# Linear attention in a fused decoder layer: one function table for exp and log, softplus in one VectorE operation, two biases on TensorE, the division on GpSimd

## The chip, the cores and the metric

One core of one Trainium2 chip runs the whole program. The metric is the device time of one execution in microseconds (us), median of several runs. A difference of about 0.2% can be told from no change. Engines: TensorE (PE, its weight loads PEld), VectorE (DVE), ScalarE (ACT), GpSimd (POOL), SyncE (SP), which issues most DMAs.

## The reference

A decoder layer over x (64 sequences of 128 rows of 128 features, float32): linear attention, cross attention to a context, and a mixture of experts, each followed by add and layer norm. The change touches the linear attention alone:

```
q = softplus(x @ Wq.T + bq);  k = softplus(x @ Wk.T + bk);  v = x @ Wv.T + bv      # 16 heads of 8
kv = cumsum(k[:, :, None] * v[:, None, :]);  k1 = cumsum(k)                        # over the 128 rows
out = (q . kv) / (q . k1)
x = layernorm(x + out @ Wo.T + bo)
```

softplus(z) is computed as max(z, 0) + log(1 + exp(-|z|)).

## The kernel before

The three layers are three blocks, one after the other. The linear attention (L153 to L483) works through 32 steps of two sequences (u = 0, 1), software-pipelined by hand: in step t an engine works for pair t, t-1, t-2, t-3 or t-4, by what it does. Each engine has its own instruction list (`step` in its block); the lists meet by semaphores, and within a list the order is that of the code. X keeps the whole activation in SBUF; x_rows is a second copy of x, loaded pair by pair (L245), for the matmuls.

In step t

- TensorE turns x_rows (L436), multiplies by Wq and Wk with the bias in front as two matmuls of a row of ones with the bias, split in a high and a low float32r part (L442, L443, then the float32 matmul L444, 256 columns; per u), turns the attention output of pair t-3 (L450), makes v of pair t (L459) and the output projection of pair t-3 (L464, both 128 columns per u, into one PSUM bank ps_vy), then the running sums of pair t-1 by a triangular matrix: of k (L472) and of kv (L479, four matmuls of 512 columns). The hardware runs each float32 matmul as two records in the profile.
- ScalarE copies the turned x out of PSUM (L307), writes the two normalised outputs of pair t-4 (L310), copies the turned attention output (L322), then |z| (L327), exp (L330), max(z, 0) (L332, into pos) and log (L335) of pair t, and the copy of v (L339). Exp and log need different function tables, so the program holds an ACT_TABLE_LOAD ahead of each.
- VectorE multiplies q by the sums (L356, once per u), adds pos and log to qk (L368), computes the shift of the layer norm (L374), the denominators' product (L380), the sums over the head dimension (L385), the residual (L390, projection plus X), the reciprocal of the denominators (L395), the layer norm's statistics (L399, L409, L413, L415) and the division, a product with the reciprocal (L403, into att).
- GpSimd computes the power of -0.5 (L267), adds the output bias to X (L272) and the value bias to v (L275), and makes the products k*v (L283, once per u).

At step 5 SyncE also issues the loads of all later weights (L134 to L149), ahead of the x_rows of pair 6 (L245).

Of the kernel before, what the change touches and what calls it, by code (L numbers as in the profile page):

```python
# [152 lines left out]
def linear_attention(nc, X, lat, ident, tri, x, weights, biases, later):  # L153
# [11 lines left out]
    with ExitStack() as stack:  # L165
# [5 lines left out]
        b_v = room.sbuf("b_v", [P, D])  # L171
        ones = room.sbuf("ones", [1, P], F32R)
        b_o = room.sbuf("b_o", [P, D])
        x_rows = room.sbuf("x_rows", [P, 2, 2, D])
        turned = room.sbuf("turned", [P, 4, S])
        pos = room.sbuf("pos", [P, 2, 2 * QK])
# [35 lines left out]
        pos_ready, v_ready, vb_ready = room.sem("pos_ready"), room.sem("v_ready"), room.sem("vb_ready")  # L212
# [5 lines left out]
        bias_added, sum_ready = room.sem("bias_added"), room.sem("sum_ready")  # L218
# [35 lines left out]
        def _(pool):  # L254
# [3 lines left out]
            pool.wait_ge(bvo_loaded, 32)  # L258
            for n in range(4):
                pool.wait_ge(res_loaded[n], 16)  # L260

            def step(t, par):
                s1, s4 = t - 1, t - 4
                if here(s4):
                    pool.wait_ge(square_ready, s4 * 2 + 2)
                    wait(pool, x1_ready, s4 * 2 - 2)
                    nc.gpsimd.tensor_tensor(scale[:, par, :], square[:, par, :], half[:], ALU.pow  # L267
                                            ).then_inc(scale_ready, 1)
                if here(s1):

                    pair = X[:, bass.ds(s1 * 2 * D, 2 * D)]
                    nc.gpsimd.tensor_tensor(pair.rearrange("p (b d) -> p b d", b=2), pair.rearrange("p (b d) -> p b d", b=2),  # L272
                                            b_o[:].unsqueeze(1).broadcast_to([P, 2, D]), ALU.add).then_inc(bias_added, 1)
                    pool.wait_ge(v_ready, s1 + 1)
                    nc.gpsimd.tensor_tensor(v[:, 1 - par], v[:, 1 - par], b_v[:].unsqueeze(1).broadcast_to([P, 2, D]),  # L275
                                            ALU.add).then_inc(vb_ready, 1)
                    pool.wait_ge(vb_ready, s1 + 1)
                    pool.wait_ge(qk_ready, s1 + 1)
                    for u in range(2):
                        wait(pool, cum_psum, s1 * 2 - 1 + u)  # L280
                        k_u = qk[:, 1 - par, u, D:QK].rearrange("p (h d) -> p h d", h=H)
                        v_u = v[:, 1 - par, u].rearrange("p (h e) -> p e h", h=H)
                        nc.gpsimd.tensor_tensor(kv[:, u], k_u.unsqueeze(1).broadcast_to([P, E, H, E]),  # L283
                                                v_u.unsqueeze(3).broadcast_to([P, E, H, E]), ALU.mult
                                                ).then_inc(kv_ready, 1)
# [4 lines left out]
        def _(act):  # L290
# [3 lines left out]
            for b, n in ((b_v, 2), (b_o, 3)):  # L294
                act.dma_start(b[:], biases[n].rearrange("(o d) -> o d", o=1).broadcast_to([P, D])
                              ).then_inc(bvo_loaded, 16)
            for n in range(4):
                act.dma_start(X[:, n * QUART * D:(n + 1) * QUART * D].rearrange("s (b d) -> s b d", d=D),
                              x[n * QUART:(n + 1) * QUART].rearrange("b s d -> s b d")).then_inc(res_loaded[n], 16)
            act.wait_ge(wT_psum, 1)  # L300
            nc.scalar.copy(w[:], ps_t[:]).then_inc(wT_ready, 1)

            def step(t, par):
# [19 lines left out]
                if here(t):  # L323
# [7 lines left out]
                    wait(act, qk_ready, t - 1)  # L331
                    nc.scalar.activation(pos[:, par], ps_qk[:], ACT.Relu).then_inc(pos_ready, 1)  # L332
# [11 lines left out]
        def _(dve):  # L344
# [4 lines left out]
                                    ).then_inc(b_lo_ready, 1)  # L349

# [9 lines left out]
            def step(t, par):  # L360
# [3 lines left out]
                if here(s1):  # L364

                    dve.wait_ge(log_ready, s1 + 1)
                    wait(dve, den_psum, s1 - 1)
                    nc.vector.tensor_tensor(qk[:, 1 - par].rearrange("p u f -> p (u f)"), pos[:, 1 - par], log[:], ALU.add  # L368
                                            ).then_inc(qk_ready, 1)
# [16 lines left out]
                if here(s3):  # L386
                    dve.wait_ge(vy_psum, t + 1)
                    dve.wait_ge(bias_added, s3 + 1)
# [11 lines left out]
                if here(s2):  # L400
                    dve.wait_ge(inv_ready, s2 + 1)
                    wait(dve, aT_psum, s2)
                    nc.vector.tensor_tensor(att[:].rearrange("p u h e -> p u e h"), numden[:, :, 0:E, :],  # L403
                                            inv[:].unsqueeze(2).broadcast_to([P, 2, E, H]), ALU.mult
                                            ).then_inc(att_ready, 1)
# [15 lines left out]
        def _(pe):  # L421
# [5 lines left out]
            pe.wait_ge(b_lo_ready, 1)  # L427
            pe.wait_ge(ones_ready, 1)

            def step(t, par):  # L430
                s1, s3 = t - 1, t - 3
                if here(t):
# [6 lines left out]
                    wait(pe, pos_ready, t)  # L439
# [17 lines left out]
                if here(t):  # L457
                    for u in range(2):
                        last = nc.tensor.matmul(ps_vy[:, u * D:(u + 1) * D], turned[:, u, :], w[:, QK:3 * D],  # L459
                                                start=True, stop=True)  # L460
                if here(s3):
                    pe.wait_ge(aT_ready, s3 + 1)
                    for u in range(2):
                        last = nc.tensor.matmul(ps_vy[:, (2 + u) * D:(3 + u) * D], turned[:, 2 + u, :], w[:, 3 * D:4 * D],  # L464
                                                start=True, stop=True)
# [953 lines left out]
```

## Time and profile before

| | us |
|---|---|
| median of 3 runs (lowest, highest) | 2271.53 (2271.13, 2274.04) |
| the profiled execution | 2267.62 |
| its span on the core | 2265.6 |
| granted TensorE clock, mean over the span | 0.985 |

| engine | busy us (share of the span) |
|---|---|
| PE | 2163.8 (96%) |
| PEld | 1841.5 (81%) |
| DVE | 1575.9 (70%) |
| ACT | 1479.8 (65%) |
| POOL | 1386.0 (61%) |

The linear attention takes the first 322 us or so of the span; the cross attention starts its first matmul at 324.3 us. The shares above are means over three layers with different limits, so what the change is worth has to be read from the first 322 us alone. A clock of 1.0 is the 2.4 GHz level of TensorE, 0.5 the 1.2 GHz level.

### The profile page before, as it was taken

What the parts mean: (1) busy time and instruction counts of PE and PEld (TensorE: products, weight loads), DVE (VectorE), ACT (ScalarE), POOL (GpSimd) and SP (SyncE); (2) the same over time, 40 slices, a digit from 0 to 9 for tenths busy, and PEclk for the clock granted to TensorE, in tenths of its full rate; (3) what the DMA queues carried; (4) which work ended last, traced back from release to release, by engine and by line L of the source; (5) the groups of instructions that cost most, each with busy time, mean ns of one, the idle gap of its engine ahead of it and who ended that gap; (6) DMA issues with size and microseconds to landing.
All of it is one profiled execution on the core that took longest, in us unless ns stands there. A gap on an engine that the chain in (4) does not pass through costs nothing. (4 is left out here: it accounts for less than half of the span.)

```text
span 2265.6 us, 44642 instructions
## 1 busy us (share of the span) xinstructions
PE 2163.8 (96%) x16233; PEld 1841.5 (81%) x16233; DVE 1575.9 (70%) x3455; ACT 1479.8 (65%) x3820; POOL 1386.0 (61%) x1481
## 2 busy tenths in 40 slices
PE   6899967999999999999999999999989999999998
PEld 3455547999999999999999999999977777777776
DVE  3899965666666666666666666666657777777775
ACT  4788845667676666666676766666655665665664
POOL 4788856566565565565665655655654666666666
PEclk9999979999999999999999999999999999999999
DMA  3311110000000000000000000000000000000000
GB/s 93 113 33 33 30 30 5 6 10 6 10 7 6 10 6 6 11 6 6 11 6 10 7 6 10 6 6 10 6 1 1 10 5 10 10 5 10 10 5 14
DMA packets 52794, 33.46 MB, mean 15 GB/s; under 512 B 2968, under 2 KB 50274, under 8 KB 52450
## 3 DMA queue, kind: packets, MB, share of 16 engines
q1 hardware_dynamic: 50174, 26.30, 4.0%
q10 hardware_dynamic: 2404, 4.33, 0.7%
q8 instruction: 131, 2.15, 0.4%
q14 instruction: 85, 0.70, 0.1%
HBM read 22.22 MB, written 8.39 MB: 14 GB/s over the span
## 5 line engine op out<-in xcount | busy, mean ns | idle before, releaser
L653 POOL TENSOR_TENSOR x_prob<-x_prob,x_inv 128x496 f32<-128x496 f32 x514 | 521.7, 1015 | 546.9 <-DVE x_inv L792 546.9
L728 ACT ACTIVATE x_prob<-x_ps_S,x_nmax 128x248 f32<-128x248 f32 x1028 | 473.2, 468 | 130.4 <-DVE x_nmax L786 130.3
L786 DVE TENSOR_REDUCE x_nmax<-x_ps_S 128x2 f32<-128x496 f32 x515 | 345.5, 671 | 181.3 <-PE x_ps_S L491 181.1
L736 ACT COPY x_probT<-x_ps_T 124x512 f32<-124x512 f32 x512 | 300.7, 587 | 225.0 <-PE x_ps_T L955 225.0
L1117 POOL TENSOR_TENSOR e_hidden_lo<-e_hidden,e_hidden_hi 128x512 fp32r<-128x512 f32 x224 | 291.8, 1306 | 196.6 <-ACT e_hidden_hi L1161 195.7
L489 PE MATMUL x_ps_S<-x_kT_lo,x_G_hi 128*128 128x248 f32 x1030 | 329.6, 320 | 0.0
L955 PE MATMUL x_ps_T<-ident,x_prob 128*124 128x128 f32 x2048 | 315.1, 276 | 11.3 <-POOL x_prob L653 11.3
L955 PEld LDWEIGHTS x_ps_T<-ident,x_prob 128*124 128x124 f32 x2048 | 237.8, 139 | 71.7 <-POOL x_prob L653 29.2
L490 PE MATMUL x_ps_S<-x_kT_hi,x_G_lo 128*128 128x248 f32 x1030 | 287.3, 279 | 0.0
L491 PE MATMUL x_ps_S<-x_kT_hi,x_G_hi 128*128 128x248 f32 x1030 | 286.7, 278 | 0.0
L772 DVE TENSOR_TENSOR x_G_lo<-x_ps_G,x_G_hi 128x512 fp32r<-128x512 f32 x259 | 178.8, 690 | 129.2 <-ACT x_G_hi L722 129.1
L930 PE MATMUL x_ps_O<-x_probT,x_V 124*64 124x128 f32 x4096 | 251.8, 276 | 0.2 <-ACT x_probT L736 0.2
L930 PEld LDWEIGHTS x_ps_O<-x_probT,x_V 124*64 124x64 f32 x4096 | 220.9, 137 | 18.9 <-issue 5.1
L1172 ACT ACTIVATE e_silu<-e_ps_gate 128x512 f32<-128x512 f32 x224 | 134.5, 601 | 154.5 <-PE e_ps_gate L491 149.0
L722 ACT CAST x_G_hi<-x_ps_G 128x512 fp32r<-128x512 f32 x259 | 152.0, 587 | 91.6 <-PE x_ps_G L491 91.4
L728 ACT ACTIVATION_READ_ACCUMULATOR x_prob<-x_ps_S,x_nmax 128x1 f32 x1028 | 206.8, 201 | 0.0
L490 PEld LDWEIGHTS x_ps_S<-x_kT_hi,x_G_lo 128*128 128x128 f32 x1030 | 196.3, 191 | 0.0
L489 PEld LDWEIGHTS x_ps_S<-x_kT_lo,x_G_hi 128*128 128x128 f32 x1030 | 195.4, 190 | 0.0
L491 PEld LDWEIGHTS x_ps_S<-x_kT_hi,x_G_hi 128*128 128x128 f32 x1030 | 194.8, 189 | 0.0
L1257 DVE TENSOR_TENSOR e_act_up<-e_silu,e_ps_up 128x512 f32<-128x512 f32 x176 | 120.3, 684 | 90.2 <-PE e_ps_up L491 52.8
L778 DVE COPY x_V<-x_ps_V 124x512 f32<-124x512 f32 x259 | 176.6, 682 | 1.8 <-PE x_ps_V L491 1.8
L1161 ACT CAST e_hidden_hi<-e_hidden 128x512 fp32r<-128x512 f32 x224 | 137.4, 613 | 26.7 <-DVE e_hidden L1263 25.9
(199 smaller groups left out, 5135.3 us busy)
## 6 DMA issues: line engine op xcount, KB each, us to landing
x_nk<-latents SPq DMA_DIRECT2D x34, 124.0 KB
lin_x_rows<-in_x SPq DMA_DIRECT2D x32, 128.0 KB, 2.4
latents<-lin_nlat SPq DMA_DIRECT2D x32, 128.0 KB, 1.8
out_dram<-e_result SPq DMA_DIRECT2D x16, 256.0 KB, 2.2
x_nk<-in_ctx SPq DMA_DIRECT2D x34, 120.0 KB, 2.1
w_wkv<-in_L_xattn_Wkv SPq DMA_DIRECT2D x1, 1024.0 KB, 6.1
w_rows<-in_L_ffn_w_gate SPq DMA_DIRECT2D x1, 704.0 KB, 5.8
w_rows<-in_L_ffn_w_up SPq DMA_DIRECT2D x1, 704.0 KB, 6.2
```

What stands on the lines that cost most here:

```text
L489: nc.tensor.matmul(out, stationary[0], moving[1], start=first, stop=False)
L490: nc.tensor.matmul(out, stationary[1], moving[0], start=False, stop=False)
L491: return nc.tensor.matmul(out, stationary[0], moving[0], start=False, stop=last)
L653: nc.gpsimd.tensor_tensor(prob[:, k], prob[:, k], inv[:, k].unsqueeze(2).broadcast_to([P, 2, K]), ALU.mult).then_inc(prob_ready, 1)
L728: nc.scalar.activation(prob[:, k, h, :], ps_S[:, n % BANKS, h * K:(h + 1) * K], ACT.Exp, bias=nmax[:, k, h:h + 1], accum_out=total[:, k, h ...
L736: nc.scalar.copy(probT[0:KT, s % (2 * GANG)], ps_T[0:KT, s % 2, :]).then_inc(probT_ready, 1)
L772: nc.vector.tensor_tensor(G_part[1][:, pair].rearrange("p h u q -> p (h u q)"), ps_G[:], G_part[0][:, pair].bitcast(F32).rearrange("p h u ...
L778: nc.vector.tensor_copy(V[:, hf, u, tile, :], ps_V[0:KT, :]).then_inc(V_ready, 1)
L786: nc.vector.tensor_reduce(nmax[:, k, :], ps_S[:, n % BANKS, 0:2 * K].rearrange("p (h k) -> p h k", h=2), AX, ALU.max, negate=True).then_in ...
L930: last = nc.tensor.matmul(ps_O[h * DH:(h + 1) * DH, k * S:(k + 1) * S], V[:, j // 4, u, tile, (j % 4 * 2 + h) * DH:(j % 4 * 2 + h + 1) * D ...
L955: last = nc.tensor.transpose(ps_T[0:KT, s % 2, at:at + S], prob[:, s % RINGS, h, tile * KT:(tile + 1) * KT], ident[:])
L1117: nc.gpsimd.tensor_tensor(hidden_part[1][0:rows, n % RING, :], hidden[0:rows, n % 2, :], hidden_part[0][0:rows, n % RING, :].bitcast(F32), ...
```

## The change

1. ScalarE: one table that holds both exp and log is loaded ahead of the steps; the max(z, 0) pass (pos) is dropped.
2. VectorE: qk is one scalar_tensor_tensor, max(ps_qk, 0) + log, read straight from PSUM. TensorE's next product into ps_qk therefore waits for qk and not for pos.
3. The value and output biases leave GpSimd. They become two small matmuls per sequence (a row of ones by a 128-column part of the bias, high and low) ahead of each product, in the new `projected`. The two extra biases are split in the prologue on VectorE, which also waits for X there.
4. The division moves from VectorE in step t (pair t-2) to GpSimd in step t+1 (the same pair, now t-3), ahead of the power.

```diff
@@ -168,12 +168,11 @@
-        b_v = room.sbuf("b_v", [P, D])
+        b_vo = room.sbuf("b_vo", [1, 2, D])
+        b_vo_part = [room.sbuf(f"b_vo_{n}", [1, 2, D], F32R) for n in ("hi", "lo")]
-        b_o = room.sbuf("b_o", [P, D])
-        pos = room.sbuf("pos", [P, 2, 2 * QK])
...
@@ -255,26 +254,22 @@
             nc.gpsimd.memset(half[:], -0.5).then_inc(half_ready, 1)
             nc.gpsimd.memset(ones[:].bitcast(F32), 1.0).then_inc(ones_ready, 1)
             pool.wait_ge(half_ready, 1)
-            pool.wait_ge(bvo_loaded, 32)
-            for n in range(4):
-                pool.wait_ge(res_loaded[n], 16)
 
             def step(t, par):
-                s1, s4 = t - 1, t - 4
+                s1, s3, s4 = t - 1, t - 3, t - 4
+                if here(s3):
+                    pool.wait_ge(inv_ready, s3 + 1)
+                    wait(pool, aT_psum, s3)
+                    nc.gpsimd.tensor_tensor(att[:].rearrange("p u h e -> p u e h"), numden[:, :, 0:E, :],
+                                            inv[:].unsqueeze(2).broadcast_to([P, 2, E, H]), ALU.mult
+                                            ).then_inc(att_ready, 1)
                 if here(s4):
                     pool.wait_ge(square_ready, s4 * 2 + 2)
                     wait(pool, x1_ready, s4 * 2 - 2)
                     nc.gpsimd.tensor_tensor(scale[:, par, :], square[:, par, :], half[:], ALU.pow
                                             ).then_inc(scale_ready, 1)
                 if here(s1):
-
-                    pair = X[:, bass.ds(s1 * 2 * D, 2 * D)]
-                    nc.gpsimd.tensor_tensor(pair.rearrange("p (b d) -> p b d", b=2), pair.rearrange("p (b d) -> p b d", b=2),
-                                            b_o[:].unsqueeze(1).broadcast_to([P, 2, D]), ALU.add).then_inc(bias_added, 1)
                     pool.wait_ge(v_ready, s1 + 1)
-                    nc.gpsimd.tensor_tensor(v[:, 1 - par], v[:, 1 - par], b_v[:].unsqueeze(1).broadcast_to([P, 2, D]),
-                                            ALU.add).then_inc(vb_ready, 1)
-                    pool.wait_ge(vb_ready, s1 + 1)
                     pool.wait_ge(qk_ready, s1 + 1)
                     for u in range(2):
                         wait(pool, cum_psum, s1 * 2 - 1 + u)
@@ -291,12 +286,12 @@
             for n in range(2):
                 act.dma_start(b_qk[:, n * D:(n + 1) * D], biases[n].rearrange("(o d) -> o d", o=1)
                               ).then_inc(bqk_loaded, 16)
-            for b, n in ((b_v, 2), (b_o, 3)):
-                act.dma_start(b[:], biases[n].rearrange("(o d) -> o d", o=1).broadcast_to([P, D])
-                              ).then_inc(bvo_loaded, 16)
+            for n in range(2):
+                act.dma_start(b_vo[:, n, :], biases[2 + n].rearrange("(o d) -> o d", o=1)).then_inc(bvo_loaded, 16)
             for n in range(4):
                 act.dma_start(X[:, n * QUART * D:(n + 1) * QUART * D].rearrange("s (b d) -> s b d", d=D),
                               x[n * QUART:(n + 1) * QUART].rearrange("b s d -> s b d")).then_inc(res_loaded[n], 16)
+            nc.scalar.preload_act_table_set("natural_log_exp_and_others")
             act.wait_ge(wT_psum, 1)
             nc.scalar.copy(w[:], ps_t[:]).then_inc(wT_ready, 1)
 
@@ -328,8 +323,6 @@
                     act.wait_ge(mag_ready, t + 1)
                     wait(act, log_ready, t)
                     nc.scalar.activation(dec[:], mag[:], ACT.Exp, scale=-1.0).then_inc(dec_ready, 1)
-                    wait(act, qk_ready, t - 1)
-                    nc.scalar.activation(pos[:, par], ps_qk[:], ACT.Relu).then_inc(pos_ready, 1)
                     act.wait_ge(dec_ready, t + 1)
                     wait(act, qk_ready, t)
                     nc.scalar.activation(log[:], dec[:], ACT.Ln, bias=1.0).then_inc(log_ready, 1)
@@ -347,6 +340,13 @@
             dve.wait_ge(b_hi_ready, 1)
             nc.vector.tensor_tensor(b_qk_part[1][:], b_qk[:], b_qk_part[0][:].bitcast(F32), ALU.subtract
                                     ).then_inc(b_lo_ready, 1)
+            dve.wait_ge(bvo_loaded, 32)
+            nc.vector.tensor_copy(b_vo_part[0][:], b_vo[:]).then_inc(b_hi_ready, 1)
+            dve.wait_ge(b_hi_ready, 2)
+            nc.vector.tensor_tensor(b_vo_part[1][:], b_vo[:], b_vo_part[0][:].bitcast(F32), ALU.subtract
+                                    ).then_inc(b_lo_ready, 1)
+            for n in range(4):
+                dve.wait_ge(res_loaded[n], 16)
 
             def numerators(s, par, u):
 
@@ -365,8 +365,8 @@
 
                     dve.wait_ge(log_ready, s1 + 1)
                     wait(dve, den_psum, s1 - 1)
-                    nc.vector.tensor_tensor(qk[:, 1 - par].rearrange("p u f -> p (u f)"), pos[:, 1 - par], log[:], ALU.add
-                                            ).then_inc(qk_ready, 1)
+                    nc.vector.scalar_tensor_tensor(qk[:, 1 - par].rearrange("p u f -> p (u f)"), ps_qk[:], 0.0, log[:],
+                                                   ALU.max, ALU.add).then_inc(qk_ready, 1)
                 if here(s4):
 
                     dve.wait_ge(scale_ready, s4 + 1)
@@ -385,7 +385,6 @@
                     nc.vector.tensor_reduce(numden[:], prod[:], AX, ALU.add).then_inc(numden_ready, 1)
                 if here(s3):
                     dve.wait_ge(vy_psum, t + 1)
-                    dve.wait_ge(bias_added, s3 + 1)
                     wait(dve, x1_ready, (s3 - 1) * 2)
                     nc.vector.tensor_tensor(res[:, 1 - par], ps_vy[:, 2 * D:4 * D].rearrange("p (u f) -> p u f", u=2),
                                             X[:, bass.ds(s3 * 2 * D, 2 * D)].rearrange("p (u f) -> p u f", u=2), ALU.add
@@ -397,12 +396,6 @@
                     wait_apart(dve, b_lo_ready, (sum_ready, s3 + 1), (mom_ready, s3 * 2))
                     for u in range(2):
                         nc.vector.bn_stats(stat[:, u, :], res[:, 1 - par, u, :]).then_inc(stat_ready, 1)
-                if here(s2):
-                    dve.wait_ge(inv_ready, s2 + 1)
-                    wait(dve, aT_psum, s2)
-                    nc.vector.tensor_tensor(att[:].rearrange("p u h e -> p u e h"), numden[:, :, 0:E, :],
-                                            inv[:].unsqueeze(2).broadcast_to([P, 2, E, H]), ALU.mult
-                                            ).then_inc(att_ready, 1)
                 if here(s3):
                     for u in range(2):
                         wait_apart(dve, b_lo_ready, (stat_ready, s3 * 2 + u + 1))
@@ -424,8 +417,14 @@
                 last = nc.tensor.transpose(ps_t[:, n * D:(n + 1) * D], w_rows[:, n, :], ident[:])
             last.then_inc(wT_psum, 1)
             pe.wait_ge(wT_ready, 1)
-            pe.wait_ge(b_lo_ready, 1)
+            pe.wait_ge(b_lo_ready, 2)
             pe.wait_ge(ones_ready, 1)
+
+            def projected(out, n, rows, weight):
+
+                nc.tensor.matmul(out, ones[:], b_vo_part[1][:, n, :], start=True, stop=False)
+                nc.tensor.matmul(out, ones[:], b_vo_part[0][:, n, :], start=False, stop=False)
+                return nc.tensor.matmul(out, rows, weight, start=False, stop=True)
 
             def step(t, par):
                 s1, s3 = t - 1, t - 3
@@ -436,7 +435,7 @@
                         last = nc.tensor.transpose(ps_t[:, u * S:(u + 1) * S], x_rows[:, par, u, :], ident[:])
                     last.then_inc(xT_psum, 1)
                     pe.wait_ge(xT_ready, t + 1)
-                    wait(pe, pos_ready, t)
+                    wait(pe, qk_ready, t)
                     for u in range(2):
                         out = ps_qk[:, u * QK:(u + 1) * QK]
                         nc.tensor.matmul(out, ones[:], b_qk_part[1][:], start=True, stop=False)
@@ -456,13 +455,11 @@
                     pe.wait_ge(sum_ready, s3)
                 if here(t):
                     for u in range(2):
-                        last = nc.tensor.matmul(ps_vy[:, u * D:(u + 1) * D], turned[:, u, :], w[:, QK:3 * D],
-                                                start=True, stop=True)
+                        last = projected(ps_vy[:, u * D:(u + 1) * D], 0, turned[:, u, :], w[:, QK:3 * D])
                 if here(s3):
                     pe.wait_ge(aT_ready, s3 + 1)
                     for u in range(2):
-                        last = nc.tensor.matmul(ps_vy[:, (2 + u) * D:(3 + u) * D], turned[:, 2 + u, :], w[:, 3 * D:4 * D],
-                                                start=True, stop=True)
+                        last = projected(ps_vy[:, (2 + u) * D:(3 + u) * D], 1, turned[:, 2 + u, :], w[:, 3 * D:4 * D])
                 if here(t) or here(s3):
                     last.then_inc(vy_psum, 1)
                 if here(s1):
```

How the instructions move. On TensorE, in one steady step, from the end of the q and k products to the sums of k (L459 and L464 before are the products for v and for the output, L425 to L427 now the two bias matmuls and the product). Before:

```order
L450 MATMUL lin_ps_t<-ident,lin_att 128x128
L459 MATMUL lin_ps_vy<-lin_w,lin_turned 128x128 [waits lin_sum_ready,lin_v_ready]
L459 MATMUL lin_ps_vy<-lin_w,lin_turned 128x128
L464 MATMUL lin_ps_vy<-lin_w,lin_turned 128x128 [waits lin_aT_ready]
L464 MATMUL lin_ps_vy<-lin_w,lin_turned 128x128
L472 MATMUL lin_ps_den<-lin_qk,tri 128x256 [waits lin_den_taken,lin_qk_ready]
```

Now, on TensorE in the same place (line numbers of the changed kernel):

```order
L425 MATMUL lin_ps_vy<-lin_b_vo_lo,lin_ones 128x128 [waits lin_sum_ready,lin_v_ready]
L426 MATMUL lin_ps_vy<-lin_b_vo_hi,lin_ones 128x128
L427 MATMUL lin_ps_vy<-lin_w,lin_turned 128x128
L425 MATMUL lin_ps_vy<-lin_b_vo_lo,lin_ones 128x128
L426 MATMUL lin_ps_vy<-lin_b_vo_hi,lin_ones 128x128
L427 MATMUL lin_ps_vy<-lin_w,lin_turned 128x128
L425 MATMUL lin_ps_vy<-lin_b_vo_lo,lin_ones 128x128 [waits lin_aT_ready]
L426 MATMUL lin_ps_vy<-lin_b_vo_hi,lin_ones 128x128
L427 MATMUL lin_ps_vy<-lin_w,lin_turned 128x128
L425 MATMUL lin_ps_vy<-lin_b_vo_lo,lin_ones 128x128
L426 MATMUL lin_ps_vy<-lin_b_vo_hi,lin_ones 128x128
L427 MATMUL lin_ps_vy<-lin_w,lin_turned 128x128
```

Eight matmuls are added per step; the waits stay where they were.

On GpSimd, one steady step before (v of pair t-1, then its products k*v, then the power of the next step):

```order
L267 TENSOR_TENSOR lin_scale<-lin_square,lin_half 128x4 [waits lin_x1_ready,lin_square_ready]
L272 TENSOR_TENSOR X<-X,lin_b_o 128x256
L275 TENSOR_TENSOR lin_v<-lin_v,lin_b_v 128x256 [waits lin_v_ready]
L283 TENSOR_TENSOR lin_kv<-lin_qk,lin_v 128x1024 [waits lin_cum_psum,lin_qk_ready,lin_vb_ready]
L283 TENSOR_TENSOR lin_kv<-lin_qk,lin_v 128x1024 [waits lin_cum_psum]
```

The same step on GpSimd now:

```order
L263 TENSOR_TENSOR lin_att<-lin_numden,lin_inv 128x2x8x16 [waits lin_aT_psum,lin_inv_ready]
L269 TENSOR_TENSOR lin_scale<-lin_square,lin_half 128x4 [waits lin_x1_ready,lin_square_ready]
L278 TENSOR_TENSOR lin_kv<-lin_qk,lin_v 128x1024 [waits lin_cum_psum,lin_qk_ready,lin_v_ready]
L278 TENSOR_TENSOR lin_kv<-lin_qk,lin_v 128x1024 [waits lin_cum_psum]
```

The two bias additions are gone and the division stands first; the power stands between the division and the products as it stood ahead of the additions.

## Rows read from the trace of the kernel before

**Rows 1.** Busy time of each engine in one steady stretch of 60 us.

```profile
core 0: us, PE busy (x) PEld busy (x) DVE busy (x) ACT busy (x) POOL busy (x), PEclk, DMA share, GB/s
180.00:240.00 60.00, 55.16 (x213) 31.38 (x214) 59.48 (x107) 51.66 (x92) 50.77 (x37) 1.00 0.11 31
```

**Rows 2.** Timeline of one steady step, VectorE and GpSimd (start us, us, what).

```profile
212.38 1.22 DVE L356 TENSOR_TENSOR lin_prod<-lin_ps_cum,lin_qk 128x1024 f32<-128x1024 f32 x1
...
213.52 0.68 DVE L368 TENSOR_TENSOR lin_qk<-lin_pos,lin_log 128x512 f32<-128x512 f32 x1
213.55 1.24 POOL L272 TENSOR_TENSOR X<-X,lin_b_o 128x256 f32<-128x256 f32 x1
...
214.12 0.69 DVE L374 SCALAR_TENSOR_TENSOR lin_shift<-lin_mom,lin_scale 128x4 f32<-128x4 f32 x1
...
214.75 0.72 POOL L275 TENSOR_TENSOR lin_v<-lin_v,lin_b_v 128x256 f32<-128x256 f32 x1
...
215.55 4.23 POOL L283 TENSOR_TENSOR lin_kv<-lin_qk,lin_v 128x1024 f32<-128x1024 f32 x2
...
216.31 2.56 DVE L385 TENSOR_REDUCE lin_numden<-lin_prod 128x288 f32<-128x2304 f32 x1
...
219.71 0.61 DVE L403 TENSOR_TENSOR lin_att<-lin_numden,lin_inv 128x256 f32<-128x256 f32 x1
...
220.56 1.22 DVE L356 TENSOR_TENSOR lin_prod<-lin_ps_cum,lin_qk 128x1024 f32<-128x1024 f32 x1
...
221.75 1.25 DVE L368 TENSOR_TENSOR lin_qk<-lin_pos,lin_log 128x512 f32<-128x512 f32 x1
```

**Rows 3.** Timeline of TensorE, step 7 (from 86.29 to 94.42 us).

```profile
86.29 0.38 PE L436 MATMUL lin_ps_t<-ident,lin_x_rows 128*128 128x128 f32 x2
87.14 0.38 PE L442 MATMUL lin_ps_qk<-lin_b_qk_lo,lin_ones 1*128 1x256 f32 x1 [0.46 <-ACT lin_turned L307]
...
88.19 0.38 PE L442 MATMUL lin_ps_qk<-lin_b_qk_lo,lin_ones 1*128 1x256 f32 x1
88.42 0.28 PE L443 MATMUL lin_ps_qk<-lin_b_qk_hi,lin_ones 1*128 1x256 f32 x1
88.62 0.70 PE L444 MATMUL lin_ps_qk<-lin_w,lin_turned 128*128 128x256 f32 x2
89.16 0.38 PE L450 MATMUL lin_ps_t<-ident,lin_att 128*128 128x128 f32 x2
89.38 0.61 PE L459 MATMUL lin_ps_vy<-lin_w,lin_turned 128*128 128x128 f32 x4
90.00 0.71 PE L464 MATMUL lin_ps_vy<-lin_w,lin_turned 128*128 128x128 f32 x4
90.55 0.60 PE L472 MATMUL lin_ps_den<-lin_qk,tri 128*128 128x256 f32 x2
90.98 3.60 PE L479 MATMUL lin_ps_cum<-lin_kv,tri 128*128 128x512 f32 x8
94.42 0.38 PE L436 MATMUL lin_ps_t<-ident,lin_x_rows 128*128 128x128 f32 x2
```

**Rows 4.** Timeline of TensorE at the start of the last step, 31.

```profile
289.36 0.38 PE L436 MATMUL lin_ps_t<-ident,lin_x_rows 128*128 128x128 f32 x2
```

**Rows 5.** Groups of instructions, ScalarE, up to 322 us (busy us, mean ns).

```profile
L335 ACT ACT_TABLE_LOAD x32 | 41.1, 1283 | 0.6
L330 ACT ACT_TABLE_LOAD x31 | 39.8, 1283 | 0.6
```

**Rows 6.** Timeline of TensorE in the cross attention: float32r matmuls of 248 columns.

```profile
700.74 0.28 PE L490 MATMUL x_ps_S<-x_kT_hi,x_G_lo 128*128 128x248 f32 x1
700.86 0.28 PE L491 MATMUL x_ps_S<-x_kT_hi,x_G_hi 128*128 128x248 f32 x1
```

**Rows 7.** Timeline of SyncE's DMA issues around step 5 (start us, us, what).

```profile
56.09 0.50 SPq L245 DMA_DIRECT2D lin_x_rows<-in_x  x1
...
70.88 0.47 SPq L245 DMA_DIRECT2D lin_x_rows<-in_x  x1
```

**Rows 8.** Timeline of TensorE at the start of step 6.

```profile
75.06 0.66 PE L436 MATMUL lin_ps_t<-ident,lin_x_rows 128*128 128x128 f32 x2 [4.98 <-DMA lin_x_rows<-in_x]
76.18 0.58 PE L442 MATMUL lin_ps_qk<-lin_b_qk_lo,lin_ones 1*128 1x256 f32 x1 [0.46 <-ACT lin_turned L307]
```

More of the change, by code:

```diff
@@ L211, in linear_attention @@
         qk_psum, vy_psum = room.sem("qk_psum"), room.sem("vy_psum")
-        pos_ready, v_ready, vb_ready = room.sem("pos_ready"), room.sem("v_ready"), room.sem("vb_ready")
+        v_ready = room.sem("v_ready")
         mag_ready, dec_ready, log_ready = room.sem("mag_ready"), room.sem("dec_ready"), room.sem("log_ready")
@@ L217, in linear_attention @@
         numden_ready, inv_ready, att_ready = room.sem("numden_ready"), room.sem("inv_ready"), room.sem("att_ready")
-        bias_added, sum_ready = room.sem("bias_added"), room.sem("sum_ready")
+        sum_ready = room.sem("sum_ready")
         stat_ready, mom_ready = room.sem("stat_ready"), room.sem("mom_ready")
```

## Prediction

> **What bounds the kernel now.** The page first: its shares are means over three layers, so I cut out the linear attention with the windows view. In a steady 60 us VectorE is busy 59.48 us, TensorE 55.16, ScalarE 51.66, GpSimd 50.77, at clock 1.00 [rows 1]. VectorE looks like the only limit. The timeline says why it is so full: from one L356 to the next is 220.56 - 212.38 = 8.18 us, and part of that is waiting for GpSimd. L368 takes 0.68 us when it starts ahead of L272 and L272 then takes 1.24; at 221.75 it takes 1.25. L374, four elements wide, takes 0.69 and ends at 214.81, just after L272 does (213.55 + 1.24 = 214.79) [rows 2]. So two engines that both read SBUF with two inputs take turns.
>
> TensorE decides this case, though, and a busy share doesn't show how near it is to its own limit, since its records overlap. Starts do. In step 7, after a stall, every engine had caught up with its work and TensorE waits for nothing but the round trip through ScalarE's copy of x (0.46 us): that step takes 94.42 - 86.29 = 8.13 us [rows 3]. Piece by piece: turn and copy 0.85, q and k 2.02, turn 0.22, v 0.62, output 0.55, k sums 0.43, kv sums 3.44. From step 7 to step 31 there are 24 steps, (289.36 - 86.29)/24 = 8.46 us each [rows 3, 4]. The average step is thus VectorE's, and TensorE has 8.46 - 8.13 = 0.33 us of room in it. That 0.33 is all that may be added to TensorE for nothing, and all that making the others faster can win per step.
>
> **The change part by part.**
>
> *ScalarE.* 31 + 32 table loads of 1.283 us, 81 us in all, go, and the max pass with them [rows 5]: some 3.1 us of about 7.3 per step (51.66/60 x 8.46). ScalarE was not the limit; what it gives is that its copy of x is never late. The new table load in the prologue stands where one stood before. The copy's 0.85 stays in TensorE's chain, since the copy can't start before the turned x is there.
>
> *VectorE.* The division's 0.61 goes, the turns with GpSimd go at L368 (0.57 in every other step) and up to 0.55 at L374; the new qk reads PSUM, and I take the 0.68 of the old one for it. 8.46 - 0.5 - 0.3 - 0.5 is about 7.2 us per step. Splitting two more biases in the prologue lies beside the loading of X.
>
> *GpSimd.* L272 and L275 go (0.7 to 1.2 each, [rows 2]), the division comes, 256 elements like L275, so about 0.7: some 6 us per step. The division waits for the reciprocal of the step before and stands after k*v, which ends well before; queued behind it are the power and k*v. TensorE reads its result only after q and k of the same step, some 3 us in. Both have room.
>
> *TensorE.* Eight matmuls of one row by 128 columns per step. Their price is in no row as such, so I bound it. Nearest row: the same form with 256 columns. L442 to L443 is 0.23, L443 to L444 0.20; a whole sequence (two bias matmuls and L444) takes 88.19 - 87.14 = 1.05 and 89.16 - 88.19 = 0.97 [rows 3]. A float32 product of 256 columns alone takes 0.43 (L472 to L479), so a pair costs 0.62 and 0.54. That is the upper end with nothing taken off for half the columns: 4 x 0.58 = 2.3 us per step. A float32r matmul of 248 columns with the weights loaded beside another takes 0.12 [rows 6], half of that is 0.06: the lower end is 8 x 0.06 = 0.48. That the small matmuls cost nearly twice 0.12 here shows that the weight load of the row of ones isn't hidden, and that doesn't shrink with the columns. I take the pair at 0.58 less the streaming of 256 fewer columns in all, between 0.12 (one pass, rows 6) and 0.21 (two passes, as L472's 0.43 for two records of 256): 0.46 to 0.37, say 0.425, and 4 x 0.425 = 1.7 us per step. No engine hides it: these stand in TensorE's own list, and nothing below 0.48 is possible by any row here, which is already more than the 0.33 of room.
>
> The Trainium skill ("TensorE: Matmul & The Clock Gate", section "Back-to-back issue gap") gives about 81 ns for each matmul of 128 columns in a stream with its weight load. By that the eight would cost 0.65 us, and the step would be 8.78. The rows of the same form (0.20 to 0.23 for 256 columns) speak against it, as weights of one row don't seem to be pulled ahead here.
>
> *The step* becomes TensorE's: 8.13 + 1.7 = 9.83 us against 8.46, +1.37. The waits that bound steps before (for the copies, for k*v) are gone, for VectorE at 7.2 delivers early. The new wait of q and k for the old qk (instead of pos) falls due well before: qk comes 1.8 us after the first half of the kv sums, TensorE asks for it after the second half (1.7) and the turned x (0.85). SyncE is moved past nothing.
>
> **The sum.** Steps 7 to 30: 24 x 1.37 = +32.9. Step 31: +1.4. Steps 2 to 5 would bring about 5 more, but in step 6 TensorE waits 4.98 us for x_rows, which lands 75.06 - 56.09 = 18.97 us after the issue ahead of the weight loads, at step 4 [rows 7, 8]. That issue moves with step 4 by some 2 us only, so step 6 starts some 2 us late and most of the wait is used up. Step 6 itself took 86.29 - 75.06 = 11.23 us [rows 3, 8]; its matmuls are long (0.66 against 0.38) because the clock fell to 0.5 (1.2 GHz) after those idle 5 us. With about 1.5 us idle I expect it to stay at 2.4 GHz and step 6 to take 9.8: -1.4. Up to step 7 that makes +0.5. Filling and draining: the early and late steps lose table loads and gain bias matmuls; I take 0, +-3. Sum: 0.5 + 32.9 + 1.4 = +34.8. The profiled execution took 2267.6 (span 2265.6), so 2302.4; it was 3.9 below the median of the runs, so I put 2306.
>
> **The rivals.**
>
> *A, cheap bias matmuls (12%).* The weight load of the ones hides behind the product before. For it: in the cross attention such loads do hide [rows 6]. Against: [rows 3]. Step 8.61 to 8.78: 24 x 0.15 to 0.32 is +3.6 to +7.7, the start gives or takes 1: 2275 to 2280.
>
> *B, VectorE blocked by k*v (7%).* The new step has VectorE's shift right behind qk, and k*v starts on qk as well. If k*v gets in first, the shift (two SBUF inputs) waits out one product, 2.1 us (4.23/2), or both, and L356 behind it. By 2.1 VectorE needs 9.3, which hides; by 4.2, 11.4 us, +2.9 over 8.46: 24 x 2.9 is +70, 2341. Against: the shift is next on its own engine and k*v needs a semaphore; and GpSimd's list has the power ahead of k*v, so the scale is there. The Trainium skill ("SBUF — State Buffer", section "Who interferes with whom") has this rule, that issue order decides who blocks, for the whole instruction; rows 2 agree on who waits (L374 ends with L272).
>
> *C, faster (5%).* TensorE's 8.13 holds slack I don't see, as the eight matmuls fill gaps where it waits for weights or copies: the output part waits for the copy of att, the q part 0.46 us for that of x. This decides if the eight add less than 0.33 to the 8.13. At 0 the step is 8.13: -0.33 x 24 = -8, and with the start -1 to -3: 2261. For it: 0.46 us idle per step. Against: they stand behind q and k, not in that gap.
>
> *D, the table isn't shared or the loads stay (1%).* The built program holds one ahead of the steps. TensorE's sum would be the same.
>
> The forecast has the other 75%. Its own spread is the price of the eight: 1.3 to 2.3 per step gives 2296 to 2321. The range 2285 to 2321 leaves out A below, B and C. Faster or slower counts from 0.2% (4.5 us), about what a measurement of this kernel can tell: faster 0.05, same 0.04 (the low end of A), slower 0.91.
>
> **What would show it.** In the changed profile: steady starts of the x turning 9.8 us apart; L425 to L426 0.15 to 0.2 us, v and output together 2.9 instead of 1.17; VectorE's busy share in 180 to 240 down to about 45 us with idle time ended by PE, ScalarE's to about 30; no table load in the steps; no L374 over 0.2 us; the wait for x_rows in step 6 under 3 us and clock 1.0 there. The forecast is wrong if steps stay under 8.8 us (A) or if VectorE stays at 59 of 60 us (B).

## The result, and the profile after

| | before | changed |
|---|---|---|
| median us (lowest, highest), 4 runs each | 2272.78 (2271.13, 2274.05) | 2332.51 (2329.74, 2338.10) |
| profiled execution, its span | 2267.62, 2265.6 | 2331.12, 2329.4 |
| mean granted clock of the span | 0.985 | 0.976 |

The change makes the kernel slower: ratio 1.0266, 95% interval 1.0245 to 1.0288. The forecast had the sign and the engine, but put 2306 with a range up to 2321: +35 us where +60 came. One execution of e1 below, the profiled one, took 2730.38 us at a mean granted clock of 0.744; it is left out of e1's median and ratio, and no steps are read from it.

TensorE in one steady step of the changed kernel (start us, us, what), which answers to [rows 3]:

```profile
199.16 0.38 PE L435 MATMUL lin_ps_t<-ident,lin_x_rows 128*128 128x128 f32 x2
200.01 0.38 PE L441 MATMUL lin_ps_qk<-lin_b_qk_lo,lin_ones 1*128 1x256 f32 x1 [0.46 <-ACT lin_turned L302]
...
202.03 0.38 PE L449 MATMUL lin_ps_t<-ident,lin_att 128*128 128x128 f32 x2
202.34 0.32 PE L425 MATMUL lin_ps_vy<-lin_b_vo_lo,lin_ones 1*128 1x128 f32 x1
202.50 0.27 PE L426 MATMUL lin_ps_vy<-lin_b_vo_hi,lin_ones 1*128 1x128 f32 x1
202.70 0.49 PE L427 MATMUL lin_ps_vy<-lin_w,lin_turned 128*128 128x128 f32 x2
203.12 0.32 PE L425 MATMUL lin_ps_vy<-lin_b_vo_lo,lin_ones 1*128 1x128 f32 x1
...
205.38 0.60 PE L469 MATMUL lin_ps_den<-lin_qk,tri 128*128 128x256 f32 x2
205.81 3.60 PE L476 MATMUL lin_ps_cum<-lin_kv,tri 128*128 128x512 f32 x8
...
209.24 0.38 PE L435 MATMUL lin_ps_t<-ident,lin_x_rows 128*128 128x128 f32 x2
```

The step is 10.08 us. Its pieces are those of before but for two: from the first L425 to L469 now takes 3.04 us where v and output took 1.17, and the turn ahead of them 0.31 instead of 0.22. Sum: +1.96 us for eight small matmuls, 0.245 each. A second cost is seen only over several steps. Windows of TensorE's steps 17, 18 and 19, and of steps 7 to 30 together:

```profile
core 0: us, PE busy (x) PEld busy (x) DVE busy (x) ACT busy (x) POOL busy (x), PEclk, DMA share, GB/s
199.16:209.24 10.08, 9.62 (x39) 5.85 (x38) 7.46 (x15) 4.42 (x10) 5.97 (x4) 1.00 0.09 26
209.24:221.01 11.77, 11.31 (x40) 6.80 (x39) 7.46 (x15) 4.42 (x10) 5.96 (x4) 0.86 0.08 22
221.01:231.08 10.07, 9.61 (x39) 5.84 (x38) 7.45 (x15) 4.42 (x10) 5.97 (x4) 1.00 0.10 28
93.41:350.18 256.77, 245.69 (x914) 147.97 (x913) 178.92 (x335) 106.14 (x240) 143.07 (x96) 0.94 0.09 25
```

Same instructions, same order, but step 18 is 1.69 us longer because the clock was at 0.5 (1.2 GHz) for a part of it. Three windows of 1 us within it:

```profile
214.00:215.00 1.00, 1.00 (x7) 0.81 (x6) 0.00 (x0) 0.69 (x2) 0.00 (x0) 1.00 0.00 0
216.00:217.00 1.00, 1.00 (x3) 0.69 (x3) 1.00 (x5) 0.37 (x1) 0.32 (x1) 0.50 0.00 0
219.00:220.00 1.00, 1.00 (x4) 0.43 (x3) 0.44 (x1) 0.00 (x0) 0.00 (x0) 1.00 0.00 0
```

Of the 24 steps three are some 11.77 and three some 13.35 us long: 256.77 - 24 x 10.08 = 14.9 us. In each of the six the clock fell 5.1 to 6.1 us into the step, while the bias matmuls and products were running (they start at 3.2). TensorE is never idle for longer than 0.46 us in such a step. Before, the clock stayed at 1.00 from step 7 to step 30.

Where the 63.8 us of span come from: up to step 7 93.41 - 86.29 = 7.1; steps 7 to 30 38.9 for the matmuls (24 x (10.08 - 8.46)) and 14.9 for the clock; step 31 and the end 3.0.

The other engines did as forecast. VectorE waits now and its shift is short; the copies and the division are never late, for TensorE's only idle time in steps 7 to 30 is the 0.46 us a step for the turned x:

```profile
L368 DVE SCALAR_TENSOR_TENSOR lin_qk<-lin_ps_qk,lin_log 128x512 f32<-128x512 f32 x32 | 21.8, 680 | 17.5 <-ACT lin_log L328 17.5
...
L389 DVE TENSOR_TENSOR lin_res<-lin_ps_vy,X 128x256 f32<-128x256 f32 x32 | 13.6, 423 | 65.3 <-PE lin_ps_vy L427 65.3
...
L374 DVE SCALAR_TENSOR_TENSOR lin_shift<-lin_mom,lin_scale 128x4 f32<-128x4 f32 x32 | 4.9, 152 | 2.2 <-POOL lin_scale L269 2.2
```

These are groups of VectorE up to 386 us (busy us, mean ns, then idle time before and what ended it).

### The profile page after: what moved, and what is told of

It reads as the page before. It is cut to its first block and busy times, and to the rows that moved or that the text cites. A ratio compares the mean times of both kernels' runs of the same rounds, so it can differ in the third digit from the quotient of the medians.

```text
span 2329.4 us, 44993 instructions
## 1 busy us (share of the span) xinstructions
PE 2246.6 (96%) x16489; PEld 1897.6 (81%) x16489; DVE 1548.6 (66%) x3425; ACT 1385.0 (59%) x3724; POOL 1348.9 (58%) x1449
## 5 line engine op out<-in xcount | busy, mean ns | idle before, releaser
L278 POOL TENSOR_TENSOR lin_kv<-lin_qk,lin_v 128x1024 f32<-128x1024 f32 x64 | 135.1, 2130 | 93.3 <-DVE lin_qk L368 60.6
```

## The experiments

A table first; the columns "step" and "clock's extra" come from TensorE's starts in the profiled execution, steps 7 to 30, as above (median step; sum over it). The ratio is to executions of the kernel before that were made beside each experiment (their medians were 2269.5 to 2272.8 us). The code shown for an experiment is an excerpt of its edit to the changed kernel, or to the one named.

| kernel | bias matmuls for v and output | step us | clock's extra us | median us | ratio to before (95%) |
|---|---|---|---|---|---|
| before | none | 8.46 (mean) | 0 | 2272.8 | |
| changed | 8 of 1 row | 10.08 | 14.9 | 2332.5 | 1.0266 (1.0245 to 1.0288) |
| e1 | left out | | | 2257.5 | 0.9936 (0.9917 to 0.9955) |
| e2 | none, on GpSimd | 8.12 | 0.1 | 2256.6 | 0.9936 (0.9922 to 0.9951) |
| e3 | 8 of 128 rows | 8.73 | 0.1 | 2275.0 | 1.0019 (1.0009 to 1.0029) |
| e4 | 8 of 1 row, the only edit | 10.08 | 13.2 | 2334.5 | 1.0283 (1.0264 to 1.0302) |
| e5 | 8 of 32 rows | 10.08 | 12.7 | 2326.6 | 1.0249 (1.0217 to 1.0281) |
| e6 | 8 of 64 rows | 10.08 | 6.3 | 2327.9 | 1.0255 (1.0222 to 1.0287) |
| e7 | 4 of 1 row, 256 columns | 9.09 | 6.4 | 2293.8 | 1.0101 (1.0065 to 1.0137) |
| e8 | none; table the only edit | 8.16 | 0.1 | 2262.8 | 0.9965 (0.9954 to 0.9976) |
| e9 | none; e2 with two tables | 8.13 | 0 | 2260.3 | 0.9958 (0.9942 to 0.9973) |
| e10 | none; q, k bias of 128 rows | 7.58 | 0 | 2236.8 | 0.9858 (0.9842 to 0.9874) |
| e11 | none; e10, v bias folded | 7.54 | 0 | 2237.1 | 0.9860 (0.9841 to 0.9879) |
| e12 | 24 of 128 rows | 10.52 | 0 | 2328.6 | 1.0263 (1.0238 to 1.0289) |

**e1, without the bias matmuls.**

```diff
-                nc.tensor.matmul(out, ones[:], b_vo_part[1][:, n, :], start=True, stop=False)
-                nc.tensor.matmul(out, ones[:], b_vo_part[0][:, n, :], start=False, stop=False)
-                return nc.tensor.matmul(out, rows, weight, start=False, stop=True)
+                return nc.tensor.matmul(out, rows, weight, start=True, stop=True)
```

> The changed kernel with the eight bias matmuls of v and output left out (so the value and output biases are missing). Theory 1 (the eight one-row matmuls cost about 1.95 us per step in TensorE's list, and they are also why its clock falls in the steady steps): steps of 8.13 us, no fall of the clock between step 7 and step 31, about 2258 us. Theory 2 (the clock falls because of the other parts, such as the new wait for qk or the division on GpSimd): steps of 8.13 us with several longer ones, 2270 or more.

2257.5 us: the eight matmuls make the whole 75 us to the changed kernel.

**e2, the biases back on GpSimd.** `projected` without its bias matmuls, and in GpSimd's list again:

```diff
+                    nc.gpsimd.tensor_tensor(pair..., pair..., b_o[:].unsqueeze(1).broadcast_to([P, 2, D]), ALU.add).then_inc(bias_added, 1)
                     pool.wait_ge(v_ready, s1 + 1)
+                    nc.gpsimd.tensor_tensor(v[:, 1 - par], v[:, 1 - par], b_v[:].unsqueeze(1).broadcast_to([P, 2, D]),
+                                            ALU.add).then_inc(vb_ready, 1)
```

> The changed kernel with the two biases back on GpSimd, as before the change; table, softplus and division as changed. Theory 1: TensorE's own 8.13 us per step, no fall of the clock, about 2260 us, faster than before by 0.5%. Theory 2 as for e1: 2270 or more. If VectorE's turns with GpSimd come back (L374), VectorE needs some 7.8 us, which still hides.

Windows of its steps 7 to 30:

```profile
85.21:280.20 194.99, 183.51 (x722) 108.00 (x720) 178.52 (x337) 103.61 (x240) 176.35 (x144) 1.00 0.12 33
```

8.12 us per step, TensorE's own limit as read from step 7 of before, at clock 1.00. Three parts of the change are good for 0.6%; the fourth costs about 3.4%. Theory 2 (another part lowers the clock) falls.

**e3, the same bias matmuls over 128 rows.** Bias tiles of 128 rows, zero but for the first, by a full tile of ones:

```diff
-        b_vo_part = [room.sbuf(f"b_vo_{n}", [1, 2, D], F32R) for n in ("hi", "lo")]
+        b_vo_part = [room.sbuf(f"b_vo_{n}", [P, 2, D], F32R) for n in ("hi", "lo")]
+        ones_all = room.sbuf("ones_all", [P, P], F32R)
```

> The changed kernel with the value and output biases as matmuls over all 128 rows (127 of them zero in the bias, ones in the weights): as many matmuls and columns, 128 rows instead of 1. If the one-row form is what keeps weight loads from hiding and what the clock counts as idle: 8.13 + 8 x 0.06 to 0.12 = 8.6 to 9.1 us per step, no fall of the clock in steps 7 to 31, 2275 to 2290 us. If small matmuls as such are the cause: 10.08 us per step with the same falls, 2332 us.

TensorE's timeline of it:

```profile
206.45 0.38 PE L453 MATMUL lin_ps_t<-ident,lin_att 128*128 128x128 f32 x2
206.59 0.30 PE L429 MATMUL lin_ps_vy<-lin_b_vo_lo,lin_ones_all 128*128 128x128 f32 x1
206.73 0.27 PE L430 MATMUL lin_ps_vy<-lin_b_vo_hi,lin_ones_all 128*128 128x128 f32 x1
206.84 0.44 PE L431 MATMUL lin_ps_vy<-lin_w,lin_turned 128*128 128x128 f32 x2
207.04 0.30 PE L429 MATMUL lin_ps_vy<-lin_b_vo_lo,lin_ones_all 128*128 128x128 f32 x1
```

A sequence (two bias matmuls and the product) takes 0.45 us, with one row 0.78. The step is 8.73, so eight of them add 0.61, 0.076 each: less than a third of the one-row price, for 128 times the arithmetic. And no step from 7 to 30 is longer than the others.

The weight loads (PEld) show where the price sits. The changed kernel, and then this one:

```profile
202.70 0.30 PEld L427 LDWEIGHTS lin_ps_vy<-lin_w,lin_turned 128*128 128x128 f32 x2
203.12 0.18 PEld L425 LDWEIGHTS lin_ps_vy<-lin_b_vo_lo,lin_ones 1*128 1x128 f32 x1
```

```profile
206.78 0.30 PEld L431 LDWEIGHTS lin_ps_vy<-lin_w,lin_turned 128*128 128x128 f32 x2
207.01 0.19 PEld L429 LDWEIGHTS lin_ps_vy<-lin_b_vo_lo,lin_ones_all 128*128 128x128 f32 x1
```

In the changed kernel both loads start together with their matmuls (202.70, 203.12); here they start 0.06 and 0.03 us ahead of them. Within a pair the second bias matmul follows the first by 0.16 us with one row and by 0.14 with 128. The 0.33 us more per sequence lie almost whole at the two places where the row count changes: from the second bias matmul to the product 0.20 against 0.11, from the product to the next bias matmul 0.42 against 0.20. By these starts the price sits at the change between 1 and 128 rows, and "0.245 each" is this sum shared out over the matmuls; no run has more one-row matmuls in a row to test it.

**e4, the biases on TensorE alone.** The kernel before, with the two additions taken from GpSimd and `projected` and the bias split put in:

```diff
-                        last = nc.tensor.matmul(ps_vy[:, u * D:(u + 1) * D], turned[:, u, :], w[:, QK:3 * D],
-                                                start=True, stop=True)
+                        last = projected(ps_vy[:, u * D:(u + 1) * D], 0, turned[:, u, :], w[:, QK:3 * D])
```

> The kernel before with the biases on TensorE as the only edit. Theory 1: TensorE limits at 10.08 us per step, the other three parts were worth nothing beside it, 2332 us like the whole change, give or take 4. If the parts add up instead (VectorE's full list and TensorE's, one behind the other): 8.46 + 1.95 = 10.4 us per step, 2342 us or more.

10.08 us per step and 2334.5: within noise what the whole change gives. Once TensorE is the limit, the other three parts are worth nothing.

**e5 and e6, 32 and 64 rows.** As e3, with `[32, 2, D]` and `[64, 2, D]` for `[P, 2, D]`.

> The changed kernel with the value and output biases as matmuls over 32 rows (31 of them zero). Theory R (a matmul that uses only part of the array's rows can't have its weights loaded beside its neighbours, however few or many rows): step 10.08 us as with one row. If it is the count of rows, 32 lie near one row. Clock: if it falls for the slow, thin stretch of small matmuls and not for the rows in use, the falls stay as with one row (5 to 8 in the linear attention); if it follows the rows in use, fewer of them.

> The same with 64 rows (63 zero). Theory R: step 10.08 us again, since 64 rows are still part of the array. If the price goes down with the rows: between 8.73 (128 rows) and 10.08, about 9.6 us. Clock as for 32 rows.

Timeline of the one with 64 rows:

```profile
207.04 0.32 PE L429 MATMUL lin_ps_vy<-lin_b_vo_lo,lin_ones_all 64*128 64x128 f32 x1
207.20 0.27 PE L430 MATMUL lin_ps_vy<-lin_b_vo_hi,lin_ones_all 64*128 64x128 f32 x1
207.40 0.49 PE L431 MATMUL lin_ps_vy<-lin_w,lin_turned 128*128 128x128 f32 x2
207.82 0.33 PE L429 MATMUL lin_ps_vy<-lin_b_vo_lo,lin_ones_all 64*128 64x128 f32 x1
```

0.78 us per sequence, as with one row, to the hundredth: the price doesn't follow the rows, it jumps between 64 and 128. The clock falls less with 64 rows in the one profile (6.3 us of extra time against 12.7 and 14.9), but the two medians are alike (two runs each), so whether rows count for the clock stays open.

**e7, four wide ones.** One matmul per part (high, low) for both sequences:

```diff
+                both = b_vo_part[1][:, n, :].unsqueeze(1).broadcast_to([1, 2, D])
+                nc.tensor.matmul(out, ones[:], both, start=True, stop=False)
```

> The changed kernel with one bias matmul of 256 columns for both sequences where there were two of 128: four one-row matmuls per step instead of eight, the same columns. If each pair has its own price (weight loads and the change of shape, about 0.4 of the 0.49 us per pair): two pairs of 0.54 to 0.62 us = 1.2 us per step instead of 1.95, a step of 9.3 us. If the columns made the price, 10.08. With the thin stretch 0.7 us shorter I expect at most half of the clock's falls. Total 2295 to 2308 us.

```profile
204.13 0.38 PE L426 MATMUL lin_ps_vy<-lin_b_vo_lo,lin_ones 1*128 1x256 f32 x1
204.36 0.28 PE L428 MATMUL lin_ps_vy<-lin_b_vo_hi,lin_ones 1*128 1x256 f32 x1
204.56 0.71 PE L430 MATMUL lin_ps_vy<-lin_w,lin_turned 128*128 128x128 f32 x4
```

In its timeline of TensorE a pair of 256 columns takes 0.43 us and one of 128 took 0.36 (202.34 to 202.70 above). The step is 9.09 against 9.3 forecast, so two pairs of 256 columns cost 0.96 us, 0.48 each, where four of 128 cost 0.49 each: columns don't make the price. The edit halves the matmuls and the changes of row count alike, and no run separates the two. The total of 2293.8 lies just under the 2295 to 2308 that I expected, and two steps of the 24 were longer, instead of six.

**e8, the table alone.** The kernel before with one line more:

```diff
+            nc.scalar.preload_act_table_set("natural_log_exp_and_others")
```

> The kernel before with the single function table as the only edit (the max pass, the add, both biases and the division stay as before). Theory: VectorE's list with its turns with GpSimd is the limit at 8.46 us per step, so ScalarE's 2.57 us per step are worth nothing there; a start and an end that are 2 to 4 us shorter: 2268 to 2272 us. Rival: ScalarE's lateness is what makes the step (its busy 51.7 of 60 us plus waits): 8.13 us per step, 2258 us.

The rival was right about the step: 8.16 us; the total, 2262.8, lies between its 2258 and my 2268 to 2272. Why, the two timelines tell. Before (the L368 of this step is in [rows 2], 221.75 us, 1.25 long):

```profile
220.56 1.22 DVE L356 TENSOR_TENSOR lin_prod<-lin_ps_cum,lin_qk 128x1024 f32<-128x1024 f32 x1
...
221.08 0.63 ACT L335 ACTIVATE lin_log<-lin_dec 128x512 f32<-128x512 f32 x1
...
221.72 0.72 POOL L272 TENSOR_TENSOR X<-X,lin_b_o 128x256 f32<-128x256 f32 x1
```

With the one table:

```profile
218.60 0.62 ACT L336 ACTIVATE lin_log<-lin_dec 128x512 f32<-128x512 f32 x1
...
220.46 1.22 DVE L357 TENSOR_TENSOR lin_prod<-lin_ps_cum,lin_qk 128x1024 f32<-128x1024 f32 x1
...
221.59 0.68 DVE L369 TENSOR_TENSOR lin_qk<-lin_pos,lin_log 128x512 f32<-128x512 f32 x1
221.62 1.23 POOL L272 TENSOR_TENSOR X<-X,lin_b_o 128x256 f32<-128x256 f32 x1
```

Before, the log ends at 221.71 and VectorE's sum starts 0.05 us after it could have; GpSimd's addition is in by 0.03 us, and VectorE waits it out, 0.57 us. With one table the log is there 2.4 us before, VectorE is first by 0.03 us, and the long steps go: before, 11 of the 24 sums (L368) waited GpSimd's addition out like this, with the one table none. ScalarE was "not the limit" and yet decided who was first.

**e9, e2 with two tables.** The preload line taken away again.

> The kernel of e2_pool_bias (table, softplus and division as changed, biases on GpSimd: 8.13 us per step, 2256.6 us) with the single table taken away again, so two table loads per step on ScalarE. If softplus in one VectorE operation and the division on GpSimd suffice to lift VectorE's limit, TensorE still sets 8.13 us per step and the total is 2258 to 2261 us (start and end longer). If ScalarE's chain then comes late (6.7 us busy and two waits for TensorE in 8.13), steps of 8.2 to 8.5 us, 2263 or more.

8.13 us per step, 2260.3: softplus in one operation from PSUM and the division on GpSimd also reach TensorE's limit without the single table. The gains of the parts don't add up; each alone is enough (e8, e9), since TensorE's 8.13 is next.

**e10, the bias of q and k over 128 rows, on e2.**

```diff
-        b_qk_part = [room.sbuf(f"b_qk_{n}", [1, QK], F32R) for n in ("hi", "lo")]
-        ones = room.sbuf("ones", [1, P], F32R)
+        b_qk_part = [room.sbuf(f"b_qk_{n}", [P, QK], F32R) for n in ("hi", "lo")]
+        ones = room.sbuf("ones", [P, P], F32R)
```

> The kernel of e2_pool_bias with the bias of q and k, one-row matmuls already before the change, spread over 128 rows (127 zero). From the rows of e3: a full-row pair of 256 columns adds some 0.25 us to a product where the one-row pair adds 0.54 to 0.62, so TensorE needs 8.13 - 0.68 = 7.45 us per step. GpSimd (7.44 us of work and some gaps) then limits at about 7.6 us: 2243 to 2247 us.

```profile
207.44 0.38 PE L446 MATMUL lin_ps_qk<-lin_b_qk_lo,lin_ones 128*128 128x256 f32 x1 [0.46 <-ACT lin_turned L315]
207.67 0.28 PE L447 MATMUL lin_ps_qk<-lin_b_qk_hi,lin_ones 128*128 128x256 f32 x1
207.78 0.59 PE L448 MATMUL lin_ps_qk<-lin_w,lin_turned 128*128 128x256 f32 x2
...
208.88 0.38 PE L454 MATMUL lin_ps_t<-ident,lin_att 128*128 128x128 f32 x2
```

q and k take 208.88 - 207.44 = 1.44 us instead of 2.02. 7.58 us per step, 2236.8 us: 1.4% faster than before, and 6 us below what I expected, for the start gained too (step 7 begins at 77.7 us against 85.2 in e2).

**e11, the value bias folded into the output bias.**

```diff
+            nc.tensor.matmul(ps_den[:, 0:D], b_v_wide[:], w[:, 3 * D:4 * D], start=True, stop=True
+                             ).then_inc(fold_ready, 1)
```

> e10_qk_full, and the value bias folded into the output bias: the weights of the attention sum to one, so out + b_v is the same as a bias of b_v @ Wo.T + b_o, made once ahead of the steps by one matmul and one addition. GpSimd loses the addition to v (0.73 us per step, 6.7 left), TensorE stays at 7.45, VectorE needs about 7.3: steps of 7.45 us, 2238 to 2243 us, the fastest of all. If GpSimd was not the limit in e10_qk_full, the same time as that.

7.54 us per step, and the same time as e10 within the runs: GpSimd was not the limit there: with 0.73 us of work less on it, the step is 0.04 us shorter.

**e12, 24 full-row matmuls.** `for again in range(5)` around the low part of e3.

> e3_full_rows with the low part of the value and output biases added five times instead of once (an error of four times the low part): 24 full-row matmuls of 128 columns per step instead of 8. At 0.076 us each: a step of 8.73 + 16 x 0.076 = 9.95 us, about as long as that of the changed kernel. If the clock falls because a step is long or holds many small matmuls, it falls here too (3 to 5 times in steps 7 to 31). If it falls because the array stands while the weights of part of its rows are loaded, it stays at 2.4 GHz and the total is about 2306 us.

Windows of its steps 7 to 30, and after it those of e3 and of e5 (32 rows), one fence each:

```profile
89.39:341.88 252.49, 241.41 (x1298) 170.56 (x1297) 178.96 (x337) 106.25 (x240) 143.30 (x96) 1.00 0.09 26
```

```profile
81.31:290.93 209.62, 198.54 (x914) 127.66 (x913) 179.04 (x337) 106.16 (x240) 143.21 (x96) 1.00 0.11 31
```

```profile
87.48:342.06 254.58, 243.50 (x914) 147.72 (x913) 179.10 (x337) 106.17 (x240) 143.25 (x96) 0.95 0.09 25
```

The steps are 10.52 us (0.10 per matmul, not the 0.076 of e3; the 16 added ones 0.11 each), so the total is 2328.6 and not the 2306 that I expected. They are longer than those of the changed kernel, with as much of "PE busy" (96%), and the clock is 1.00 throughout. So neither a long step nor many small matmuls of 128 rows lower it. What the kernels with falls in steps 7 to 30 (the changed one, e4, e5, e6, e7) share is bias matmuls over part of the rows beyond the four for q and k, which the kernel before had without a fall in these steps. Why these lower the clock isn't shown.

## Why the prediction was wrong

- *TensorE's room is 0.33 us per step, and the change makes TensorE the limit*: right. Its limit of 8.13 us showed in e2 and e9 to the hundredth, and the sum of its pieces gave 10.08 with the new ones.
- *The eight matmuls at 1.7 us per step*: 1.95. The pair was put at 0.425 us and costs 0.49. The 0.58 for a pair of 256 columns was too high, since e7 has 0.48 for it in this place, and what I took off for half the columns was wrong as well, since they save nothing there: two errors that partly cancel. 24 x 0.25 = 6 us.
- *The steps stay at 2.4 GHz*: this step failed most. The sum put the clock's cost at nothing because it was 1.00 before; it measured 14.9 us in steps 7 to 30. [rows 1] shows 1.00 for a list with four one-row matmuls per step, and the change trebles them (four to twelve). No row of before could have priced that; it needed a wider range upwards.
- *The start comes to +0.5 at step 7*: +7.1. The wait for x_rows did go (TensorE starts step 6 with no idle time for it, at 80.06), but the clock fell in steps 3, 5 and 6 without that idle time, so step 6 took 13.35 us where the sum had 9.8, and steps 3 and 5 lost 1.7 and 3.3. The nine falls from step 3 to step 30 make 8.2 + 14.9 = 23.1 us, against steps of 10.08: most of the 28.7 by which the sum was short.
- *End*: +3.0 with step 31, against 1.4. Within the +-3.
- *VectorE 7.2, GpSimd 6, ScalarE never late*: right, and hidden. Busy in steps 7 to 30, divided by 24: 178.92/24 = 7.5, 6.0 and 4.4.
- *ScalarE's table loads worth nothing before*: wrong as a statement on the kernel before (e8: 8.16 for 8.46), though without effect on the sum.
- *Rival A* (loads hide): not for one row; it is what e3 is, whose 8.73 lies in the rival's 8.61 to 8.78. The 81 ns of the Trainium skill ("TensorE: Matmul & The Clock Gate", section "Back-to-back issue gap") agree with e3's 76 ns per matmul, less with e12's 100 ns, and with no one-row matmul here (245 ns). *Rival B* didn't come: L374 takes 0.15 us, always ahead of k*v. *Rival C* didn't come: the 0.46 us wait stays as it was, and the eight add 1.95 us to the 8.13.

In one sum, on the profiled executions: 2302.4 forecast, 6.0 for the price, 14.9 for the clock, 6.6 up to step 7, 1.6 at the end give 2331.5; it was 2331.1.

What stays open: why the clock falls in some steps and not in others with the same instructions, and what in the added matmuls lowers it. The rows in use, the gaps between matmuls and the changes of row count all differ between the changed kernel and e12.

## What to carry to other kernels

Find how much room an engine has by its own starts in a stretch where nothing else holds it up (here 8.13 of 8.46 us), before giving it more work: its busy share doesn't say. Between matmuls of 128 rows, a bias row as a matmul was three times cheaper over all 128 rows, zeros included, than over one row (0.076 us against 0.245), and the clock didn't fall in the steady steps of e3 and e12; better still is to keep it off the engine that limits. When parts of a change each lift the same limit, measure the one that loads the next limit by itself.

## What the runs showed of the hardware

- In a stream of 128-row matmuls, a float32r matmul of 128 columns over 1, 32 or 64 rows costs 0.245 us, over 128 rows 0.076 (e3) to 0.10 (e12). Most of the difference lies where the row count changes, where the weight load starts with its matmul and not ahead of it.
- TensorE's clock fell to 1.2 GHz with no idle time over 0.46 us ahead of it, during the stretch with such partial-row matmuls (nine times in the changed kernel's linear attention), and never in 24 steps as long with full-row ones in their place (e12, one profile).
- A lead of 0.03 us decided which of VectorE and GpSimd waited for a whole instruction of the other, both reading two inputs from SBUF (e8).
- The fastest kernels of these are e10 and e11, 2236.8 and 2237.1 us, which the runs don't tell apart. e10 has table, softplus and division as changed, value and output biases on GpSimd, the bias of q and k over 128 rows.
